# Seventeen groups of experts moved into the batches of the second attention, their outputs copied out of PSUM by ScalarE

## The reference

```python
x = x + attn_a(layernorm(x))   # causal, 16 heads of 8, scores * tril / exp(n), no softmax
x = x + ffn(layernorm(x))      # 16 experts, top 2 of a token, capacity 1280 slots of an expert
x = x + attn_b(layernorm(x))   # 16 heads of 8; the keys' largest score decides the rows
x = x + ffn(layernorm(x))      # the same weights

# attn_b
scores = einsum('bhqd,bhkd->bhqk', Q, K) * scale
top_u  = top_k(scores.max(axis=-1), 6)[1]          # six queries of each head
ctx    = softmax(q_sel @ K^T * scale) @ V          # for those rows alone, zeros elsewhere
out    = scatter(ctx at top_u) @ wo.T + bo

# ffn
w, idx = top_k(softmax(xf @ router_w), 2)
rank   = cumsum(onehot(idx)) - onehot(idx)         # a token's place in its expert's buffer
xe     = x_pad[dispatch]                           # rows gathered by expert
out    = (silu(xe @ gate_w) * (xe @ up_w)) @ down_w * w
combined[token] += out
```

## Time and profile before

| | |
|---|---|
| median of three runs | 1408.18 us (1398.48 to 1413.44) |
| the profiled execution | 1396.88 us, span 1395.1 us, mean granted clock of TensorE 0.936 |
| TensorE matmuls busy | 1239.1 us (89% of the span) |
| TensorE weight loads busy | 787.4 us (56%) |
| VectorE busy | 1042.0 us (75%) |
| GpSimd busy | 836.4 us (60%) |
| ScalarE busy | 756.4 us (54%) |
| chain that ended last, by engine | TensorE 70%, VectorE 12%, GpSimd 7%, issue 4%, DMA 2%, ScalarE 2% |
| chain that ended last, largest lines | score pairs L1897 25%, gate and up L1823 8%, gathers L564 6% |

### The profile page before, as it was taken

The page is one execution under the profiler, slowest core; times in us unless marked ns, Lnnn a source line. Parts: engine busy times, 40 slices in busy tenths (PEclk is TensorE's granted clock), DMA queues, the critical chain, the costliest instruction groups (busy, mean ns, idle before and its releaser), DMA issues.

```text
span 1395.1 us, 28372 instructions
## 1 busy us (share of the span) xinstructions
PE 1239.1 (89%) x8534; PEld 787.4 (56%) x8534; DVE 1042.0 (75%) x4462; ACT 756.4 (54%) x1901; POOL 836.4 (60%) x1246
## 2 busy tenths in 40 slices
PE   3999998996999999999999999999999999999100
PEld 1566665565898965454545445545455469888100
DVE  2899999895674458898999989989998856565322
ACT  2444444442665767666676756656676546556000
POOL 3237776777525224356777767766874445367776
PEclk9999999997999998998999989999999899999655
DMA  6845602011556520000100001011000125466522
GB/s 174 259 154 192 197 30 87 28 44 60 171 163 210 166 65 16 14 11 24 32 25 29 32 24 32 29 62 48 29 28 14 44 79 162 150 218 205 150 75 75
DMA packets 119783, 125.80 MB, mean 90 GB/s; under 512 B 15568, under 2 KB 109904, under 8 KB 119632
## 3 DMA queue, kind: packets, MB, share of 16 engines
q1 hardware_dynamic: 103248, 90.42, 20.5%
q0 software_dynamic: 16384, 33.59, 7.9%
HBM read 50.15 MB, written 73.79 MB: 89 GB/s over the span
## 4 chain that ended last, share of the span: by engine, by line
PE 70%; DVE 12%; POOL 7%; issue 4%; DMA 2%; ACT 2%; SPq 0%; POOLq 0%; ACTq 0%; DVEq 0%
PE pair L1897 25%; PE pair L1823 8%; POOL vmyg L564 6%; PE pair L1685 5%; DVE pT L1401 5%; PE bank L1709 4%; PE pair L1834 4%; PE pair L1812 2%; PE bank L1630 2%; PE bank L1624 2%; PE pair L1674 2%; DVE xs L1318 2%; PE bank L1936 1%; PE bank L1916 1%; PE pair L1695 1%
## 5 line engine op out<-in xcount | busy, mean ns | idle before, releaser
L1897 PE MATMUL pair<-kT,apart 32*128 32x512 f32 x2048 | 460.2, 672 | 3.5 <-DVE smax L1401 2.0
L1401 DVE CUSTOM_DVE_ANT_0 pT<-pair,pT 128x256 f32<-128x256 f32 x1024 | 384.2, 416 | 76.1 <-ACT pT L925 70.4
L925 ACT ACTIVATE pT<-pair 128x256 f32<-128x256 f32 x1024 | 327.0, 397 | 196.8 <-PE pair L1897 193.3
L1897 PEld LDWEIGHTS pair<-kT,apart 32*128 32x128 f32 x2048 | 192.8, 192 | 128.1 <-DVE smax L1401 78.7
L564 POOL DMA_INDIRECT vmyg<-ybufA,slg x128 | 123.7, 966 | 110.6 <-DVE smax L1401 67.9
L1823 PE MATMUL pair<-xeT,unit_w 128*128 128x256 f32 x768 | 184.6, 384 | 0.0
L564 POOL DMA_INDIRECT vmyg<-ybufB,slg x128 | 122.8, 959 | 71.3 <-DVE smax L1401 33.6
L509 POOL DMA_INDIRECT dispB<-xnf,sli x128 | 129.3, 1010 | 57.0 <-issue 35.2
L509 POOL DMA_INDIRECT dispA<-xnf,sli x128 | 130.0, 1016 | 50.9 <-issue 30.2
L1128 DVE TENSOR_TENSOR pT<-pair,causal 128x1024 f32<-128x1024 f32 x128 | 151.2, 1213 | 12.1 <-PE pair L1685 11.2
L1293 DVE TENSOR_TENSOR hid<-sg,pair 128x512 f32<-128x512 f32 x96 | 65.7, 685 | 123.3 <-ACT sg L851 123.1
(11 more groups left out here) (231 smaller groups left out, 1947.6 us busy)
## 6 DMA issues: line engine op xcount, KB each, us to landing
dispB<-zeros SPq DMA_DIRECT2D x16, 1408.0 KB
apart<-dispA SPq DMA_DIRECT2D x96, 128.0 KB
ybufA<-ye SPq DMA_DIRECT2D x48, 256.0 KB
apart<-dispB SPq DMA_DIRECT2D x96, 128.0 KB
ybufB<-ye SPq DMA_DIRECT2D x48, 256.0 KB
dispA<-zeros SPq DMA_DIRECT2D x33, 128.0 KB
xs<-in_x SPq DMA_DIRECT2D x16, 256.0 KB, 3.1
out<-xs SPq DMA_DIRECT2D x15, 256.0 KB, 2.6
```

The lines of the kernel that those rows point to most:

```text
L925: act.activation(rel[n % RING][:, q, :], pair[n % RING][:, q, HALF:SEQ], ACT.Relu).then_inc(s["relu_done"], 1)
L1401: dve.tensor_tensor_reduce(out=rel[n % RING][:, q, :], in0=pair[n % RING][:, q, 0:HALF], in1=rel[n % RING][:, q, :], scale=1.0, scalar=LOW ...
L1897: pe.matmul(pair[n % RING][:, q, :], apart[h][at, j, t * P:(t + 1) * P], kTs[h][at, HALF:], start=True, stop=True).then_inc(s["bsc_done"], 1)
```

## The change

**Where groups stand.** Segment 1 stops at group `M1` = 13, and its last 11 groups move into batches 0 to 5 of the second attention, two a batch (batch 5 has one). Segment 2's first `M2` = 6 groups move into batches 13, 14 and 15, two a batch. Segment 2 itself starts at group 6 and has 18.

**How a group stands in a batch.** Each takes two buffers of the ring that the score pairs use. Behind the first pair of `PLACES` (pair 1 or 13) stands down of the group before in the one bank of a ring buffer, and behind the next pair the four transposes in the other. Behind the second (pair 4 or 16) stands gate in the one bank of a second ring buffer, and behind the next pair up in the other. A list `RING_OF`, made ahead, gives every pair and group its number in the ring, and the waits go by what had the buffer before (`ring_free`). Last, `TAIL` is the down of the last of the eleven groups, in batch 5.

**Who does what.** In the batches ScalarE copies both the transposed rows and the outputs (`expert_x`, `expert_y`) out of PSUM and takes silu, VectorE has the product alone (`expert_hidden`), and GpSimd copies the weights at the end of the batch before (`copies`). In the segments VectorE copies the outputs, as before. The rows of moved groups come into two buffers of their own, `xw`, for which `whose` (routing) has half its size.

**What goes with it.** The additions and statistics of batch 1 move from segment 1 to the start of batch 0. The turn and queries of batch 0 stand two pieces earlier, and its key projection behind segment 1's last group. In batch 0 the turn and query projection of the next batch stand at pairs 11 and 13, not 7 and 9. In segment 2 pieces count from its first group, and the last ones move together: turn 12, logits 13, ranks 14, counts 15, table rows 16 (13, 14, 16, 17 and 19 before). SyncE's loads and stores are written in the new order, with the wait for the sends still ahead of segment 2's last three stores.

```diff
+M1 = 13
+M2 = 6
+PLACES = ((1, 4), (13, 16))
+for _i, _g in enumerate(range(M1, GRP)):
+    WITHIN.setdefault(_i // 2, []).append((GRP + _g, *PLACES[_i % 2]))
+TAIL = ((GRP - M1) // 2, PLACES[(GRP - M1) % 2][0])
+for _i in range(M2):
+    WITHIN.setdefault(B - M2 // 2 + _i // 2, []).append((2 * GRP + _i, *PLACES[_i % 2]))
...
 # TensorE
+            def ring_free(r, q):
+                if r < RING:
+                    return
+                what, k = RING_OF[r - RING]
+                if what == "pair":
+                    pe.wait_ge(s["bmax_done"], 2 * k + q + 1)
+                elif what == "gate" and q == 0:
+                    pe.wait_ge(s["silu_done"], k + 1)
+                elif what == "gate":
+                    pe.wait_ge(s["hid_done"], k + 1)
+                elif q == 0:
+                    if what == "turn":
+                        pe.wait_ge(s["xeT_ready"], k + 1)
+                else:
+                    pe.wait_ge(s["y_ready"], k + 1)
...
                 for n in range(PAIRS):
-                    scores(b, h, n, not last)
+                    scores(b, h, n)
+                    for k in turned_in(b, n):
+                        down_beside(k - 1, TURN_AT[k])
+                    if (b, n) == TAIL:
+                        down_beside(2 * GRP - 1, TAIL_AT)
+                    for k in turned_in(b, n - 1):
+                        turn_beside(k)
+                    for k in gated_in(b, n):
+                        gate_beside(k)
+                    for k in gated_in(b, n - 1):
+                        up_beside(k)
...
 # ScalarE
                     first_half_above(b, n)
+                    for k in gated_in(b, n):
+                        expert_silu(k, pair[GATE_AT[k] % RING][:, 0, :])
+                    for k in turned_in(b, n):
+                        if k != 2 * GRP:
+                            expert_y(k - 1, pair[TURN_AT[k] % RING][:, 1, :])
...
+                    for k in turned_in(b, n - 1):
+                        expert_x(k, pair[TURN_AT[k] % RING][:, 0, :])
...
 # VectorE
                     largest(b, h, n)
+                    for k in gated_in(b, n - 1):
+                        dve.wait_ge(s["up_done"], GATED.index(k) + 1)
+                        expert_hidden(k, pair[GATE_AT[k] % RING][:, 1, :])
+                    if not last and n == 0:
+                        add_first(1, 1)
+                    if not last and n == 1:
+                        add_second(1, 1)
+                    if not last and n == 2:
+                        dve.wait_ge(s["combined"], 2)
+                        row_stats(CALLS + 1, (1,))
+                    if not last and n == 3:
+                        row_aggregates(CALLS + 1, TB)
...
 # GpSimd, at the end of a batch
+                for k, _, _ in WITHIN.get(b + 1, ()):
+                    copies(k // GRP, k % GRP)
...
 # VectorE, segment 2 (TensorE's pieces move alike)
+                if g == 13:
+                    route_max(b + B, bank[0])
                 if g == 14:
-                    route_max(b + B, bank[0])
+                    route_top(b + B)
                 if g == 15:
-                    route_top(b + B)
+                    route_ranks(b + B, bank[0])
+                    table_counts(3, bank[0])
                 if g == 16:
-                    route_ranks(b + B, bank[0])
-                if g == 17:
-                    table_counts(3, bank[0])
-                if g == 18:
                     table_starts(3)
                     table_rows(3)
-                if g == 19:
                     table_copy(3, bank[0])
```

More of the change, by code:

```diff
@@ L684, in body @@
             def body(b, u, h, x, last=True, next=True, fetch_=True, before=True):
-                if not next:
-                    for g in range(NX):
-                        copies(2, g)
                 def pair_made(n):
@@ L724, in body @@
                     normed(b + 2, b + 2 + B, xnb[(x + 2) % 4], "att", 0, att_call(b + 2))
+                for k, _, _ in WITHIN.get(b + 1, ()):
+                    copies(k // GRP, k % GRP)
+                if not next:
+                    copies(2, M2)
+                    copies(2, M2 + 1)
                 send_tile(26, 2)
```

347 lines of the change are left out of this document (219 added, 128 removed).

## The result

The kernel after took 1452.1 us in the median of four runs (1446.5 to 1458.0) against 1404.6 for the kernel before (four runs). The ratio is 1.0334 with a 95% interval of 1.0253 to 1.0415. So it is slower by 47.6 us: the direction was forecast, the size was not. The forecast was 28 us on the profiled execution, 1430 in all, and the time stands at the very end of the range of 1399 to 1452, outside the likeliest case's own 1415 to 1445.

The account below looks back on a forecast made before the run. TensorE bounds expert stages, TensorE and VectorE nearly the second attention, GpSimd's gathers the end. -33.5 + 67.7 - 6.5 + 0.5 = +28 on the profiled 1396.9 gives 1425; allowing for the median of runs, 1430 us, range 1399 to 1452.

Parts of the forecast that it names:

- the likeliest case: Forecast case in which each moved group adds 2.9 to 4.3 us to the attention: 1415 to 1445 us, chance 0.53.
- Part 1, segment 1: Segment 1 stops after 13 groups, eleven leave at 3.06 us each, so attention starts 33.5 us earlier.
- Part 2, the groups in a batch: Groups in the attention's batches: 3.8 us more in the first place, 4.1 in the second, +67.7 in all.
- the sentence on ScalarE: In the batches, ScalarE's three copies a group lie under the following pair's 1.06 us and cost nothing.
- Part 3, the clock: In the attention, a denser TensorE would spend less time at 1.2 GHz: -6.5 us, between 0 and -13.
- The price of 0.36 a microsecond: Time lost in the attention per microsecond at the lower clock level, 0.36 us, taken from batch 3.
- Part 4, segment 2: Six groups leave segment 2, but the last batch's chain through its sends decides: +0.5 us, bounds -4 and +4.
- the tail: From GpSimd's first late gather to the end: 167.5 us of gathers, unchanged whatever TensorE does in segment 3.
- late weights: Rival: GpSimd's weight copies don't fit in the batches and gates wait 1 to 2 us a batch: 1445, chance 0.06.
- That TensorE is half free: Rival: in the attention a group costs only VectorE's product, 0.6 us: 1365 to 1376 us, chance 0.14.
- That segment 2 gives its time back: Rival: segment 2's 18 us are gained in full: 1407 to 1418 us, chance 0.05.
- That the clock alone made the kernel slow: Rival from the experiments: groups cost what they save and only the low clock slows the kernel; no chance given.

Follow-up runs that it names:

- e1_table: Kernel after, with a one-column exponential behind pair 17's relu in batches holding groups, loading the table ahead: 1444.9 us, ratio 1.0306 to the kernel before.
- e7_stores: Kernel after, with segment 2's last three stores put ahead of SyncE's wait for the last batch's sends: ratio 1.0391 to the kernel before.
- e6_gate2: Kernel after, with the gate matmuls of the groups in the batches made twice into the same bank: one run, 1487.2 us.
- e3_seg2: Kernel after with only segment 2's six groups in the attention, segment 1 as before (M1 = 24): 1435.3 us, ratio 1.0251 to the kernel before.
- e12_table_last: Kernel after, with a one-column exponential loading the table ahead at pair 17 in the last batch alone: 1446.7 us, ratio 1.0321 to the kernel before.

## Why the prediction was right and where it was wrong

**Part 1, segment 1: right.** -33.5 forecast, -33.75 measured from the segment's start to the first scores.

**Part 2, the groups in a batch: right where it was worked out, and short of one term.** In batch 3, from pair 0 to the query projection (604.74 to 618.33, before 695.29 to 705.08) the growth is 13.59 - 9.79 = 3.80, forecast 3.8. TensorE's rows there, in the kernel after:

```profile
604.74 1.29 PE L2053 MATMUL pair<-kT,apart 32*128 32x512 f32 x8
605.99 1.13 PE L1933 MATMUL pair<-unit_w,hid 128*128 128x128 f32 x8
607.05 1.21 PE L2053 MATMUL pair<-kT,apart 32*128 32x512 f32 x4
608.20 0.66 PE L1914 MATMUL pair<-ident,xw 128*128 128x128 f32 x4
608.78 1.13 PE L2053 MATMUL pair<-kT,apart 32*128 32x512 f32 x4
...
611.21 1.13 PE L1920 MATMUL pair<-xeT,unit_w 128*128 128x256 f32 x4
612.27 1.13 PE L2053 MATMUL pair<-kT,apart 32*128 32x512 f32 x4
613.33 1.13 PE L1920 MATMUL pair<-xeT,unit_w 128*128 128x256 f32 x4
...
618.33 1.13 PE L2001 MATMUL bank<-xnT,b_wq 128*128 128x512 f32 x2
```

Single pairs take 1.05 to 1.15 between insertions, and there is no gap. From there to the selected scores (632.61) it is 14.28, before 10.27: 4.01, forecast 4.1. Then to the transposes at 638.18 5.57, before 4.52: 1.05, forecast nothing. The three are 8.86 of the batch's 8.87. The step that failed is the sentence on ScalarE, that its work "cost nothing while it has 12 us a batch free": its copies did, but the change of tables that silu brings did not. The load stands ahead of an exponential whose result TensorE then waits for. Over the attention the groups cost 78.8 us at equal clock (687.1 - 608.3) where 67.7 was forecast, and e1_table took 8.3 of these 11.1 away (with 0.36, 7.1 of 7.9). That is 4.4 to 4.6 a group, above the forecast's 2.9 to 4.3.

**Part 3, the clock: wrong, sign and size.** -6.5 was forecast from a denser TensorE. The attention had 98.9 us at 1.2 GHz for 52.7, some 13 us at 0.29. The price of 0.36 a microsecond was near: the runs of the kernel after with mean clocks of 0.918 and 0.929 differ by 11.5 us, about 0.35 for each of the 32 to 34 us more at the lower level. What failed is the premise: TensorE had no gap in the two places, but the late exponential made one, and in the last batch that cost 8 us or so more. That batch had 34.1 us at the lower clock, before 6.8. Batches 8 to 12, which hold no groups, had 47.7, before 3.4, and batches 0 to 7 had 17.0, before 38.9, in one execution each; neither is explained.

**Part 4, segment 2: right in its sum in this execution, not in its picture.** +0.5 forecast, -0.2 measured, and the first late gather in the forecast span of 96 to 102 us. The six other kernels with the groups moved stand 2.5 to 5.0 above the kernel before there, from the last score to the end. TensorE was to wait some 8 us; it was idle for 20. The places of the last batch came 70.9 us behind the last score, where 68.9 was worked out, and 2 us were won back between the last send and the first gather (14.7 us, before 17.1). And the tail was taken as GpSimd's alone, "whatever TensorE does in segment 3". e7_stores shows that a first gather 9.6 us earlier gains nothing, because the index copies of segment 3 came only 2.4 us ahead of the gather that needs them.

**The number.** 1452.1 is inside the range by luck: the range reached that far for late weights, and no gate waited for weights. What filled the place was the table switch and the clock, neither of which the sum had as a cost.

**The rivals.** That TensorE is half free fell with e6_gate2: weight loads are busy half the time in batch 3 (23.27 of 47.16 us), and a matmul more costs its full time. The Trainium skill's Trainium Kernel Development and Optimization, Reading a trace, calls weight-load busy share a good measure of how close a kernel is to roofline. Read as free room, as that rival did, it would have made the matmul free; the measurement decides against this reading for a stretch in which 128 of 240 matmuls use 32 rows. That segment 2 gives its time back fell with e3_seg2. That the clock alone made the kernel slow falls with the table: at equal clock 78.8 of the attention's 92.2 us are left.

## What to carry over

Before work moves beside other work, list the functions that ScalarE will then alternate between: a switch cost 1.28 us each time here, at a place that nobody wrote down, on an engine that was idle for a third of the batch, and a one-column call a few microseconds ahead puts it where the engine waits anyway. A stage whose buffers form a short ring pays for what it must hold as well as for what it must compute, so cutting an insertion in pieces can be cheaper than keeping it whole. And where a tail starts behind a wait, ask what the second wait is before counting on the first. A forecast that lands in its range is checked part by part: here one term of the sum was missing, and two executions of a kernel differ by more than some of the terms.

## What the runs showed of the hardware

An idle gap of 0.99 us on TensorE, at one place of the last batch, went with 20 to 31 us at 1.2 GHz in seven kernels of seven, one execution each; in six kernels without it no stretch that long began there, and in e12_table_last, with that gap alone taken away, none did. The same gap elsewhere was followed by one in 5 cases of 67. Between executions of one kernel the mean granted clock differs (0.923 to 0.937 in eleven runs of the kernel before, with 1392.8 us at the highest and about 1408 at the lowest), so differences under half a per cent are read from the traces here and not from the times. The load of a table took 1.283 us, and the next activation started 1.30 us behind its start. A full-array matmul group between 32-row matmuls cost its whole time although weight loads were busy 49% of the batch.
